# Down projection of two feed-forward stages with the weights stationary and 512 tokens moving

## The reference, cut to what matters

```python
# layer 0 (ternary weights wu, wg, wd), x is [2, 1024, 256]
up = jnp.einsum('bsd,ed->bse', x, wu)
gate = jnp.einsum('bsd,ed->bse', x, wg)
hidden = jax.nn.silu(up) * gate
ffn = jnp.einsum('bse,de->bsd', hidden, wd)      # the down projection
x = _layernorm(x + ffn)                          # mean and variance over d
# layer 1 has the same form with w_gate, w_up, w_down in full precision
```

## Time and profile before

| what | value |
|---|---|
| median of three runs | 1231.12 us |
| span of the profiled execution | 1230.2 us (0.9 us under that median; the profile gives no other time of its own) |
| PE busy | 1079.5 us, 88% of the span |
| DVE busy | 734.5 us, 60% |
| ACT busy | 599.5 us, 49% |
| POOL busy | 205.9 us, 17% |
| mean granted TensorE clock | 0.948 |
| feed-forward of layer 0 | from 401 to 519 us |
| feed-forward of layer 1 | from 1073 us to the end |

### The profile page before, as it was taken

How to read it: one execution, slowest core, us unless ns; L and a number is a source line. 1 busy time by engine, 2 the same in 40 slices (tenths; PEclk the granted TensorE clock), 3 DMA queues, 4 the chain that set the end, 5 groups by cost and what they waited for, 6 DMA issues and landing times. The chain is left out here.

```text
span 1230.2 us, 22020 instructions
## 1 busy us (share of the span) xinstructions
PE 1079.5 (88%) x7890; PEld 608.7 (49%) x7890; DVE 734.5 (60%) x1451; ACT 599.5 (49%) x1169; POOL 205.9 (17%) x248
## 2 busy tenths in 40 slices
PE   7857999889988999584689999998999998899996
PEld 4523333343324788541344444544454544388885
DVE  4777666677734565464966868585866753244322
ACT  3313666556665334252046666665666664632221
POOL 1041111111111344205042000000000000032332
PEclk9957999989999999786889999999999999999998
DMA  7583323334000000019530303303030000000001
GB/s 263 124 152 42 48 38 39 38 53 53 2 1 1 1 1 1 17 52 171 63 102 8 49 17 36 46 8 54 2 52 4 2 2 1 1 1 18 1 18 35
DMA packets 28484, 49.72 MB, mean 40 GB/s; under 512 B 5639, under 2 KB 21895, under 8 KB 25916
## 3 DMA queue, kind: packets, MB, share of 16 engines
q1 hardware_dynamic: 26540, 43.46, 20.5%
q0 software_dynamic: 1008, 3.52, 0.8%
q10 hardware_dynamic: 816, 1.18, 0.3%
HBM read 35.56 MB, written 12.32 MB: 39 GB/s over the span
## 5 line engine op out<-in xcount | busy, mean ns | idle before, releaser
L787 ACT ACTIVATE prob<-ps 128x512 f32<-128x512 f32 (+6 forms) x896 | 450.5, 535 | 356.0 <-PE ps L839 343.4
L730 DVE TENSOR_REDUCE negm<-ps 128x1 f32<-128x512 f32 (+3 forms) x896 | 484.0, 608 | 160.6 <-PE ps L811 159.2
L839 PE MATMUL ps<-qop,kop 98*128 98x512 bf16 (+15 forms) x1376 | 313.4, 292 | 51.3 <-ACT prob L787 34.1
L811 PE MATMUL ps<-kop,qop 96*128 96x128 bf16 (+11 forms) x1120 | 300.5, 331 | 47.0 <-DMA qturn<-in_qturn 17.9
L839 PEld LDWEIGHTS ps<-qop,kop 107*128 107x128 bf16 (+2 forms) x1376 | 111.0, 99 | 257.5 <-ACT prob L787 205.8
L870 PE MATMUL ps<-prob,vst 128*32 128x512 f32 (+4 forms) x1792 | 211.9, 545 | 0.0
L811 PEld LDWEIGHTS ps<-kop,qop 105*128 105x128 bf16 (+1 forms) x1120 | 103.1, 101 | 125.5 <-DVE negm L730 47.6
L1229 PE MATMUL ps<-xs,ffn_parts 128*128 128x512 f32 x640 | 150.5, 392 | 4.5 <-DVE hf L1203 2.3
L1229 PEld LDWEIGHTS ps<-xs,ffn_parts 128*128 128x128 f32 x640 | 119.0, 188 | 29.8 <-DVE hf L1203 3.1
L1151 POOL TENSOR_TENSOR hs<-hf,hs 128x512 fp32r<-128x512 f32 x64 | 82.4, 1291 | 171.1 <-ACT hs L1168 170.6
L1249 PE MATMUL ps<-ffn_parts,hs 128*128 128x256 f32 x640 | 82.7, 293 | 7.9 <-POOL hs L1151 7.9
(11 more groups left out here) (102 smaller groups left out, 818.5 us busy)
## 6 DMA issues: line engine op xcount, KB each, us to landing
qop<-q_parts SPq DMA_DIRECT2D x96, 128.0 KB, 7.1
kop<-k_parts SPq DMA_DIRECT2D x48, 128.0 KB, 7.9
kop<-k_parts SPq DMA_DIRECT2D x48, 96.0 KB
q_parts<-qop SPq DMA_DIRECT2D x8, 384.0 KB, 3.0
q_parts<-kop SPq DMA_DIRECT2D x8, 384.0 KB, 6.6
x<-in_x SPq DMA_DIRECT2D x4, 512.0 KB, 7.2
out<-x SPq DMA_DIRECT2D x4, 512.0 KB, 2.9
k_parts<-qop SPq DMA_DIRECT2D x4, 384.0 KB, 2.6
```

What stands on the lines that cost most here:

```text
L730: nc.vector.tensor_reduce(negm[:, lo // CH, h, qt:qt + 1], ps[:, S_BANK + k % S_SLOTS, lo % CH:lo % CH + hi - lo], AX.X, ALU.max, negate=T ...
L787: nc.scalar.activation(prob[0:rows, q % 2, k % HG, lo % CH:lo % CH + hi - lo], ps[0:rows, T_BANK + k % 2, lo % CH:lo % CH + hi - lo], ACT. ...
L811: return nc.tensor.matmul(ps[:, S_BANK + k % S_SLOTS, a % CH:a % CH + b - a], lhs, rhs, start=start, stop=True, skip_group_check=True)
L839: return nc.tensor.matmul(ps[0:rows, T_BANK + k % 2, a % CH:a % CH + b - a], lhs, rhs, start=start, stop=True, skip_group_check=True)
```

## The change

The operands of the down projection are exchanged. The stationary operand is now a 128x128 block of the down weights, and all 512 tokens of the chunk move through it: 32 matmuls of 512 columns in layer 0 and 48 in layer 1. The result is transposed: features on the partitions, tokens along the columns, one PSUM bank for each half d of the 256 features. So it has to be turned back. ACT copies bank 4 and DVE bank 5 into a new SBUF tile `dt` (`copy_down`), PE transposes eight 128x128 blocks into the same two banks (`back`), and only then does DVE add.

The steps after it are moved to later units: the copies to e = 2, PE's `back(c - 1)` after unit 8c + 3, the additions from e = 1 to e = 4, POOL's inverse from e = 3 to e = 5, and DVE's normalisation from e = 5 to e = 6. Two pairs of semaphores are merged into others, to make room for three new ones: `mean_done` into `stat` and `eps_done` into `rstd`.

```diff
-            dve.wait_ge(self.stat[second], t + 1)
-            nc.vector.bn_aggr(self.mv[:, second, t, :], self.stats[:, second, t, :]).then_inc(self.mean_done[second], 1)
+            dve.wait_ge(self.stat[second], CT * c + t + 1)
+            nc.vector.bn_aggr(self.mv[:, second, t, :], self.stats[:, second, t, :]).then_inc(self.stat[second], 1)
...
-                if e == 3 and c >= 1:
+                if e == 5 and c >= 1:
                     prep.inverse(pool, c - 1, 1)
...
+            def copy_down(c):
+
+                act.wait_ge(down_full, 2 * c + 1)
+                if c >= 1:
+
+                    act.wait_ge(back_full, 2 * c)
+                nc.scalar.copy(dt[:, 0, :], ps[:, 4, :]).then_inc(down_act, 1)
...
+                if c >= 1 and e == 2:
+                    copy_down(c - 1)
             round_hidden(NC * KE - 1)
+            copy_down(NC - 1)
...
+                nc.vector.tensor_copy(dt[:, 1, :], ps[:, 5, :]).then_inc(down_dve, 1)
...
-                    dve.wait_ge(down_full, 2 * c + half + 1)
+                    dve.wait_ge(back_full, 2 * c + half + 1)
...
-                if c >= 1 and e == 1:
+                if c >= 1 and e == 2:
+                    copy_down(c - 1)
+                if c >= 1 and e == 4:
                     add_second(c - 1)
-                if c >= 1 and e == 5:
+                if c >= 1 and e == 6:
                     prep.normalise(dve, c - 1, 1)
+            copy_down(NC - 1)
             add_second(NC - 1)
...
+                for d in range(KD):
+                    if c >= 1:
+
+                        pe.wait_ge(prep.added[1], 2 * (c - 1) + d + 1)
+                    n = 0
+                    for e in range(KE):
+                        for a, b in pairs:
+                            last = nc.tensor.matmul(ps[:, 4 + d, :], wdown[a][:, e, d * P:(d + 1) * P],
+                                                    hs[:, e, b, :], start=(n == 0), stop=(n == KE * len(pairs) - 1))
+                            n += 1
+                    last.then_inc(down_full, 1)
+
+            def back(c):
+
+                pe.wait_ge(down_act, c + 1)
+                pe.wait_ge(down_dve, c + 1)
                 for half in range(2):
                     for j in range(2 * half, 2 * half + 2):
-                        n = 0
-                        for e in range(KE):
-                            for a, b in pairs:
-                                last = nc.tensor.matmul(ps[:, 4 + half, (j % 2) * D:(j % 2 + 1) * D],
-                                                        hs[:, e, b, j * P:(j + 1) * P], wdown[a][:, e, :],
-                                                        start=(n == 0), stop=(n == KE * len(pairs) - 1))
-                                n += 1
-                    last.then_inc(down_full, 1)
-
+                        for d in range(KD):
+                            last = nc.tensor.transpose(ps[:, 4 + half, (j % 2) * D + d * P:(j % 2) * D + (d + 1) * P],
+                                                       dt[:, d, j * P:(j + 1) * P], K.ident[:])
+                    last.then_inc(back_full, 1)
...
                     unit(u)
+                    if c >= 1 and u == c * KE + 3:
+                        back(c - 1)
                 down(c)
+            back(NC - 1)
```

More of the change, by code:

```diff
@@ L979, in __init__ @@
         self.stat = [sem(f"stat{tag}{s}") for s in range(2)]
-        self.mean_done = [sem(f"mean_done{tag}{s}") for s in range(2)]
-        self.eps_done = [sem(f"eps_done{tag}{s}") for s in range(2)]
         self.rstd = [sem(f"rstd{tag}{s}") for s in range(2)]
@@ L1038, in mean_and_variance @@
         for t in range(CT * c, CT * c + CT):
-            dve.wait_ge(self.stat[second], t + 1)
-            nc.vector.bn_aggr(self.mv[:, second, t, :], self.stats[:, second, t, :]).then_inc(self.mean_done[second], 1)
+            dve.wait_ge(self.stat[second], CT * c + t + 1)
+            nc.vector.bn_aggr(self.mv[:, second, t, :], self.stats[:, second, t, :]).then_inc(self.stat[second], 1)
     def normalise(self, dve, c, second):
         nc, x = self.nc, self.K.x
-        dve.wait_ge(self.rstd[second], c + 1)
+        dve.wait_ge(self.rstd[second], 2 * c + 2)
         for t in range(CT * c, CT * c + CT):
@@ L1053, in inverse @@
         tiles = slice(CT * c, CT * c + CT)
-        pool.wait_ge(self.mean_done[second], CT * (c + 1))
+        pool.wait_ge(self.stat[second], 2 * CT * (c + 1))
         nc.gpsimd.tensor_scalar(self.inv[:, second, 0, tiles], self.mv[:, second, tiles, 1], LN_EPS, 0.0, ALU.add,
-                                ALU.add).then_inc(self.eps_done[second], 1)
-        pool.wait_ge(self.eps_done[second], c + 1)
+                                ALU.add).then_inc(self.rstd[second], 1)
+        pool.wait_ge(self.rstd[second], 2 * c + 1)
         nc.gpsimd.tensor_tensor(self.inv[:, second, 1, tiles], self.inv[:, second, 0, tiles], self.K.power[:],
@@ L1116, in feed_forward @@
     down_full = sem("down_full" + tag)
+    down_act = sem("down_copied_act" + tag)
+    down_dve = sem("down_copied_dve" + tag)
+    back_full = sem("down_back" + tag)
     stored = sem("stored" + tag)
@@ L1128, in feed_forward @@
         hf = sb(st, "hf" + tag, [P, 2, CH], F32)
+        dt = sb(st, "dt" + tag, [P, KD, CH], F32)
         w = K.wffn
@@ L1168, in round_hidden @@
                 nc.scalar.copy(hs[:, e, 0, :], hf[:, u % 2, :]).then_inc(h_hi, 1)
+            def copy_down(c):
[3 more added lines that the diff above has]
+                nc.scalar.copy(dt[:, 0, :], ps[:, 4, :]).then_inc(down_act, 1)
             for u in range(NC * KE):
+                c, e = u // KE, u % KE
                 act.wait_ge(up_full, u + 1)
@@ L1180, in _, with copy_down @@
                     prep.act(act, what, k)
+                if c >= 1 and e == 2:
+                    copy_down(c - 1)
             round_hidden(NC * KE - 1)
+            copy_down(NC - 1)
         @block.vector
         def _(dve):
+            def copy_down(c):
+                dve.wait_ge(down_full, 2 * c + 2)
+                if c >= 1:
+                    dve.wait_ge(back_full, 2 * c)
+                nc.vector.tensor_copy(dt[:, 1, :], ps[:, 5, :]).then_inc(down_dve, 1)
             def add_second(c):
```

## The result

| | median us | lowest to highest | runs |
|---|---|---|---|
| before | 1230.49 | 1229.65 to 1233.09 | 4 |
| changed | 1249.41 | 1242.90 to 1253.73 | 4 |

The ratio of changed to before is 1.0137, with a 95% interval of 1.0109 to 1.0166, so 13 to 20 us slower. The forecast was 1243.2 us and 1238 to 1248. The direction is right and the size too small: 12 us were forecast, and the interval begins at 13. Put on the 1231.1 us from which the forecast counts, the ratio gives 1248.0 us, the upper end of the range; the median itself lies above it. The execution in the profile is the fastest of the four, 1242.9 us with a span of 1240.8; it shows less of the loss than the median does.

What follows compares the result with a forecast made beforehand. PE was taken as the bound, plus everything between the last unit and the last instruction. Matmuls -3.3, moved work with hidden turning back +12.1, last down projections -0.7, ends +4.0: +12.1 on 1231.1, so 1243.2 us, range 1238 to 1248.

Steps and rivals of the forecast that it cites:

- Matmuls: Down projections, first three chunks of both stages: 512-column matmuls at 0.227 us gain 0.5 or 0.6 a chunk, -3.3 us.
- Moved layer norm work: Feed-forward chunks of both layers: later additions and normalisation delay products and down projections; with six hidden `back` calls, +12.1 us.
- The 2.35 us of a normalisation beside one low part: DVE's four normalisations beside one POOL low part, taken halfway between 1.38 us alone and 3.32 beside two.
- Turning back: Eight PE transposes take 0.87 us; six of eight `back` calls lie inside PE's stream, 5.2 us.
- Ends: After each stage's last down projection: copy, first four transposes, an addition and handovers, +2.05 us layer 0, +1.95 layer 1.
- clock terms: Half-clock loss in the last down projections: 2.7 us kept in layer 0, 2.2 taken in layer 1.
- the rival with 1245.5 us: Clock falls once more, after PE's 2.8 us wait in layer 0's chunk 2, costing another 1.8 to 2.7 us; chance 0.20.

Runs made afterwards that it cites:

- the one with e = 7: Changed kernel with DVE normalising chunk c - 1 after unit e = 7 instead of e = 6: 1237.17 us, ratio 1.0045 to before.
- the last waits filled: Changed kernel plus 30 (layer 0) and 20 (layer 1) extra matmuls between unit 31 and the last down projection: 1246.34 us, again 1246.79.
- the last chunk multiplied directly: Changed kernel with normalisation at e = 7, each stage's last chunk using the old down projection, without copy or turning back: 1234.58 us, ratio 1.0018.

## Why the prediction was right in direction and short in size

**Matmuls.** Forecast 7.26 and 10.9 us a chunk; measured 7.38 and 10.9. The rate of 0.227 was right in layer 1; in layer 0 it was 0.231, so a chunk gained 0.4 and not 0.5 us.

**Moved layer norm work.** From the first unit after a down projection to the next down projection, in layer 0: chunk 1 forecast 22.1, measured 22.33 (429.67 to 452.00); chunk 2 20.15 and 20.14 (459.39 to 479.53); chunk 3 19.35 and 19.49 (487.42 to 506.91). In layer 1 the last one was forecast at 21.3 to 22.2 and came at 22.1, the upper end: POOL's low part 30 and the normalisation started together, and the first normalisation instruction waited for it. The 2.35 us of a normalisation beside one low part was 2.31. Reading the order of four engines against the rows gave the starts of the down projections to 0.3 us in layer 0; the waits themselves were 2.44 for 2.8 and 7.11 for 7.5 us. Over both stages the chunks between the down projections grew by 13.0 us, turning back included, where 12.1 was forecast; the largest miss is the last one of layer 1, +3.0 for the 2.5 that I took. That the moves make the waits is shown by the kernel with the moves alone and by the one with e = 7.

**Turning back.** Eight transposes took 0.87 us, as forecast. Inside the stream PE waited for a copy only in chunk 1 of layer 0 (0.30 us, as forecast).

**Ends.** Forecast 1.95 us in layer 1. Measured: from the end of the down projection to the first statistics 2.82 us (1230.19 to 1233.01) against 0.72, so 2.1. With the two last down projections, whose clock terms were kept, the ends came to +3.3 us, as forecast (4.0 - 0.7).

**The clock: the step that failed.** The sum left the clock alone in chunk 2 of layer 0. I had given the further fall a chance of 0.20, since after the wait of 2.75 us in layer 1 it had come only at the very end. In all five profiles of the changed kernel (two of them with the last waits filled) the clock fell there, though the wait was 2.4 us and not 2.8. PE waits 2.4 us, works 0.9 and waits again up to 0.8. I had set the two waits down but judged only the first; yet in two of the five the clock was already low before the first wait ended (477.2 against 477.52 in the profile shown), so the pair isn't needed for it. In the down projection behind it the fall cost 0.5, 1.3 and 2.9 us against 7.38 in the three profiles, and 0.9 and 0.5 in the filled ones. So the rival with 1245.5 us was the true case, and its price of 1.8 to 2.7 us too narrow at both ends. In layer 0's last down projection the fall cost less than I kept (9.6 us for my 9.9).

**The sum.** In the profiled execution the two stages lost 13.8 us; forecast 12.1. Of the 1.7 us too little, 0.9 are the moved work, 0.3 the matmuls of layer 0 and 0.5 the clock in chunk 2. In the other two profiles of the same kernel the stages lost 15.1 and 16.3, of which that fall has 1.3 and 2.9. So the clock is the smaller part of the miss in the first and the larger in the third. The medians lie 15.6 to 18.9 us above before. I read the profile of the fastest of four runs; no profile was taken of the two runs above 1252, so what of the first median's 18.9 us lies in the two stages and what in falls of the clock elsewhere is not known.

## What to carry to other kernels

Making a wide matmul out of two narrow ones was worth only the overhead between matmuls, here 13 ns each, and turning the transposed result back cost more than that. When a step of an in-order engine is moved to a later place, look at what then stands behind it and when its input comes: 9.9 us of this change's loss came from a normalisation put one product too early, about as much as all the copies and the turning back, and the kernel before had a milder form of the same fault. Price a wait of PE with a fall of its clock behind it, by the waits of like length in the traces and as a range. And when an execution differs from another, sum the stages that the change touches before reading the whole span.

## What the runs showed of the hardware that I had not expected

**The same wait may or may not bring the fall.** Behind a wait of 2.77 us in layer 1 the last down projection was at half clock for part of its time in four profiles (12.78 to 13.28 us: before, semaphores merged, and both kernels with the normalisation at e = 7 and no filling) and at the full clock throughout in two (11.20 us with the exchange only, 11.78 with the last chunk multiplied directly). The unfilled waits of 4.6 us and more ahead of a last down projection brought it in all thirteen cases, the 2.44 us in chunk 2 in all six. A wait of 3.03 us didn't, and two waits of 0.81 us with 0.9 of work between them did in one of six profiles. In chunk 2 of layer 0 the low stretch lasted 3.4 us in one execution and 6.8 in another.

**Scatter.** The changed kernel took 1243 to 1254 us over 16 runs. The kernel before took 1228 to 1240 in 68 of its 69 runs and 1251 in the other, so it scatters as widely, and the waits that the change adds can't be called the cause. Outside the two stages, where every kernel has the same work, the thirteen profiled executions took 952.3 to 958.6 us.

**DVE and POOL.** A normalisation of four instructions took 1.38 us alone, 2.31 us (layer 0) or 2.46 (layer 1) beside one low part of POOL and 3.32 beside two. In layer 1 of the changed kernel the first of the four took 1.49 us and the others 0.40; it began at 1211.86 and ended at 1213.35, just behind POOL's instruction, which ran from 1211.94 to 1213.20. The Trainium skill ("SBUF — State Buffer", section on the two separate sides) says that DVE's two-port operations and POOL take their shared ports as an exclusive lock for a whole instruction; these rows agree. Which of the two gets the ports they don't settle: the record has DVE starting 0.08 us ahead of POOL there, and DVE was the one that waited.
